# One attention stage of a six-stage decoder: the second norm's statistics taken from the first's, and weight splits cut in quarters

## The reference, cut to what matters

```python
def _layernorm(x, axis=-1, eps=1e-05):
    m = jnp.mean(x, axis=axis, keepdims=True)
    v = jnp.var(x, axis=axis, keepdims=True)
    return (x - m) / jnp.sqrt(v + eps)
...
x = _layernorm(x + _L0_attn_ref(x, L0_attn_Wq, L0_attn_Wk, L0_attn_Wv, L0_attn_Wo, L0_attn_scale), axis=-1)
x = _layernorm(x + _L0_xattn_ref(x, ctx_1024, L0_xattn_ln_gamma, L0_xattn_ln_beta, L0_xattn_w_q, L0_xattn_w_kv, L0_xattn_w_out, L0_xattn_b_out, L0_xattn_gate), axis=-1)
```

## Time and profile before

| what | value |
|---|---|
| median of 3 runs | 1186.19 us (1182.67 to 1187.83) |
| the profiled execution, its own time | 1185.38 us |
| its span | 1183.4 us |
| mean granted clock of TensorE | 0.961 |
| busy: PE, DVE, ACT, POOL | 1011.8, 891.5, 660.6, 567.9 us |

### The profile page before, as it was taken

How to read it: one execution, slowest core, us unless ns; L and a number is a source line. 1 busy time by engine, 2 the same in 40 slices (tenths; PEclk the granted TensorE clock), 3 DMA queues, 4 the chain that set the end, 5 groups by cost and what they waited for, 6 DMA issues and landing times.

```text
span 1183.4 us, 24998 instructions
## 1 busy us (share of the span) xinstructions
PE 1011.8 (85%) x8412; PEld 850.7 (72%) x8429; DVE 891.5 (75%) x2472; ACT 660.6 (56%) x2644; POOL 567.9 (48%) x671
## 2 busy tenths in 40 slices
PE   6998976799999999988999789977798676899984
PEld 2664655687788888767777689976687565788873
DVE  6899976677777777787777567659879566799885
ACT  5998974555555555554555354432553344666753
POOL 2677784333333333334883312758502684345452
PEclk9999988899999999999999899988999888999998
DMA  5510104400000000000111026432210110000000
GB/s 188 200 29 19 29 10 147 134 2 1 2 1 1 1 2 2 1 1 6 35 35 35 29 72 214 120 84 63 55 39 23 38 34 8 2 10 11 15 19 23
DMA packets 55604, 51.47 MB, mean 43 GB/s; under 512 B 6813, under 2 KB 48949, under 8 KB 55093
## 3 DMA queue, kind: packets, MB, share of 16 engines
q1 hardware_dynamic: 29556, 30.20, 8.0%
q10 hardware_dynamic: 21824, 11.28, 3.2%
q0 software_dynamic: 4096, 8.40, 2.5%
HBM read 29.66 MB, written 16.52 MB: 39 GB/s over the span
## 4 chain that ended last, share of the span: by engine, by line
PE 40%; DVE 27%; POOL 13%; issue 10%; ACT 6%; DMA 2%; ACTq 1%; DVEq 1%; SPq 0%; POOLq 0%
PE bank L672 34%; PE bank L687 6%; POOL xs L1752 5%; ACT PP L1466 3%; POOL GA L1770 3%; DVE X L1029 3%; DVE MX L1052 3%; POOL PP L1691 2%; DVE VB L1023 1%; DVE AC L1026 1%; DVE STA L1037 1%; ACTq L1552 1%; DVE X L1026 1%; DVE OT L1023 1%; DVE ED L1032 1%
## 5 line engine op out<-in xcount | busy, mean ns | idle before, releaser
L1466 ACT ACTIVATE PP<-bank,MX 128x128 f32<-128x128 f32 x832 | 296.2, 379 | 249.4 <-DVE MX L1052 227.1
L1691 POOL TENSOR_TENSOR PP<-PP,RS 128x512 f32<-128x512 f32 x208 | 215.8, 1045 | 219.2 <-DVE RS L1120 218.9
L1466 ACT ACTIVATION_READ_ACCUMULATOR PP<-bank,MX 128x1 f32 x832 | 178.4, 217 | 0.0
L1052 DVE TENSOR_REDUCE MX<-bank 128x4 f32<-128x512 f32 x208 | 141.1, 679 | 22.8 <-PE bank L672 18.6
L687 PE MATMUL bank<-KON,PP 128*128 128x128 f32 x832 | 135.4, 286 | 22.7 <-DVE PT L1023 13.5
L687 PEld LDWEIGHTS bank<-KON,PP 128*128 128x128 f32 x832 | 93.1, 143 | 58.3 <-issue 43.5
L672 PE MATMUL bank<-XST,WS 128*128 128x128 f32 x936 | 120.6, 280 | 2.8 <-ACT XST L1454 2.8
L672 PEld LDWEIGHTS bank<-XST,WS 128*128 128x128 f32 x936 | 114.0, 197 | 3.3 <-ACT XST L1454 3.3
L1023 DVE COPY PT<-bank 128x512 f32<-128x512 f32 x128 | 87.7, 685 | 12.7 <-PE bank L687 5.3
L1057 DVE COPY WS<-WCt 128x1152 f32 x78 | 64.6, 829 | 39.2 <-PE bank L672 28.7
L1752 POOL DMA_INDIRECT xs<-X,POS x64 | 67.7, 1058 | 49.8 <-DVE POS L1023 31.7
(11 more groups left out here) (259 smaller groups left out, 2472.6 us busy)
## 6 DMA issues: line engine op xcount, KB each, us to landing
xs<-BTZ ACTq DMA_DIRECT2D x2, 2496.0 KB, 18.8
XS<-xs SPq DMA_DIRECT2D x78, 64.0 KB, 1.9
ys<-YS ACTq DMA_DIRECT2D x78, 64.0 KB, 1.5
WFt<-wf SPq DMA_DIRECT2D x8, 515.0 KB, 5.0
KB<-KS SPq DMA_DIRECT2D x56, 64.0 KB, 2.0
WCt<-we SPq DMA_DIRECT2D x1, 3072.0 KB, 11.4
XT<-xT SPq DMA_DIRECT2D x8, 256.0 KB, 5.8
X<-x SPq DMA_DIRECT2D x8, 256.0 KB, 6.0
```

Source lines behind the costliest of these rows:

```text
L1052: e.tensor_reduce(m["MX"][:, u % d, :], heads(sb), AX.X, ALU.max, negate=True).then_inc(s["sm_max"], 1)
L1466: ins = e.activation(m["PP"][i][:, j, :], sb[:, one(j)], ACT.Exp, bias=m["MX"][:, i, j:j + 1], accum_out=m["SM"][:, i, j:j + 1])
L1691: return e.tensor_tensor(o, x, y, op)
```

## The change

The second norm's mean is 0, and its variance follows from the first's: with v the variance of z, the normalised row has v / (v + eps), and both norms together divide by the root of v(1 + eps) + eps². So `A_out` now makes two columns on VectorE (v + eps and v(1 + eps) + eps²), GpSimd raises both in one instruction, and one step `A_ln` writes XH and X, both from z. `A_ln2` is gone, and so are 32 `bn_stats` and 32 `bn_aggr`. The lags are now 8 (`A_out`), 10 (`A_ln`) and 12 (`A_xn`): all three fall on even i. `B_w` becomes 12 steps of a quarter (256 columns) at i = 22, 24, ... 44, `B_wv` four at i = 56 to 59, and `B_parts` 1 moves from 57 to 61. `B_wob` stays.

```diff
+WQK_AT = tuple(range(22, 46, 2))
+WV_AT = tuple(range(2 * NB - 8, 2 * NB - 4))
...
     def a_tail(i):
-        for name, lag in (("A_xn", 13), ("A_ln2", 11), ("A_ln", 9), ("A_out", 8)):
+        for name, lag in (("A_xn", 12), ("A_ln", 10), ("A_out", 8)):
...
-        if i in (27, 31, 35):
-            do("B_w", (27, 31, 35).index(i))
+        if i in WQK_AT:
+            do("B_w", WQK_AT.index(i))
...
+        if i in WV_AT:
+            do("B_wv", WV_AT.index(i))
+        if i == nu - 3:
+            do("B_parts", 1)
         if i == nu - 7:
             do("B_parts", 0)
-            do("B_wv")
-            do("B_parts", 1)
...
@@ TensorE
         elif name == "B_q":
             c, n = k
-            q.wait_ge("B_wl", 2)
+            q.wait_ge("B_wl", 8)
             q.wait_ge("B_lo", hi_lo(c)[1])
...
         elif name == "B_v":
             c, n = k
-            q.wait_ge("B_lo", max(hi_lo(c)[1], 3))
+            q.wait_ge("B_wl", 12)
+            q.wait_ge("B_lo", hi_lo(c)[1])
...
@@ VectorE
         e.bn_aggr(mv[:, 0:2], st).then_inc(s["ln_dv"], 1)
         q.wait_ge("ln_dv", 3 * n - 1)
+        if ty == "A":
+            ts(mv[:, 3:4], mv[:, 1:2], 1.0 + EPS, EPS * EPS, ALU.mult, ALU.add)
         ts(mv[:, 2:3], mv[:, 1:2], EPS, None, ALU.add).then_inc(s["ln_dv"], 1)
...
         elif name == "A_ln":
             b, = k
-            apply(X[:, b, :], X[:, b, :], "A1", b).then_inc(s["A_x1"], 1)
-            q.wait_ge("A_x1", b + 1)
-            stats("A2", b, X[:, b, :])
-        elif name == "A_ln2":
-            b, = k
+            mv = m["MVA"][:, b % 4, :]
+            q.wait_ge("ln_pw", N["A", b])
             q.wait_ge("A_xt", max(b - 3, 0))
-            apply(m["XH"][b % 4], X[:, b, :], "A2", b).then_inc(s["A_xh"], 1)
+            chain("A_xh", b + 1, ts(m["XH"][b % 4], X[:, b, :], mv[:, 0:1], mv[:, 5:6], ALU.subtract, ALU.mult))
+            ts(X[:, b, :], X[:, b, :], mv[:, 0:1], mv[:, 4:5], ALU.subtract, ALU.mult).then_inc(s["A_x1"], 1)
...
@@ ScalarE
+        elif name == "B_w" and k[0] % 3 < 2:
+            n, w = quarter(k[0] // 3), k[0] % 3
             q.wait_ge("ld_B", 96)
+            if w == 0:
+                e.activation(m["WQH"][:, n], m["WQB"][:, n], ACT.Copy, scale=0.125).then_inc(s["B_wh"], 1)
+            else:
+                cp(m["WKH"][:, n], m["WKB"][:, n]).then_inc(s["B_wh"], 1)
...
@@ GpSimd
+        if ty == "A":
+            tt(mv[:, 4:6], mv[:, 2:4], m["SW"][:, 0:2], ALU.pow).then_inc(s["ln_pw"], 1)
...
+            if w == 0:
+                q.wait_ge("B_wh", 2 * (k[0] // 3) + 1)
+                e.tensor_scalar(m["WQB"][:, n], m["WQB"][:, n], 0.125, None, ALU.mult).then_inc(s["B_wsc"], 1)
             else:
+                q.wait_ge("B_wh", 2 * (k[0] // 3) + w)
+                q.wait_ge("B_wsc", k[0] // 3 + 1)
+                x = ("WQ", "WK")[w - 1]
+                tt(m[x + "L"][:, n], m[x + "B"][:, n], m[x + "H"][:, n].bitcast(F32), ALU.subtract).then_inc(s["B_wl"], 1)
...
         elif name == "B_wv":
+            n = quarter(k[0])
+            q.wait_ge("B_wh", 9 + k[0])
+            tt(m["WVL"][:, n], m["WVB"][:, n], m["WVH"][:, n].bitcast(F32), ALU.subtract).then_inc(s["B_wl"], 1)
```

More of the change, by code:

```diff
@@ L458, in norms @@
 def norms(steps):
-    first = {"A_out": "A1", "A_ln": "A2", "B_out": "B", "combine": "C", "F_st": "F"}
+    first = {"A_out": "A", "B_out": "B", "combine": "C", "F_st": "F"}
     out = {}
@@ L590, in memory @@
         m[n] = at(n, 24)[:, :].rearrange("p (k j) -> p k j", k=6)
-    for n in ("A1", "A2", "B", "C", "D", "E", "F"):
+    m["MVA"] = at("MVA", 24)[:, :].rearrange("p (k j) -> p k j", k=4)
+    for n in ("A", "B", "C", "D", "E", "F"):
         m["ST" + n] = [at(f"ST{n}{i}", 6)[:, :] for i in range(2)]
-        m["MV" + n] = at(f"MV{n}", 16)[:, :].rearrange("p (k j) -> p k j", k=4)
+        if n != "A":
+            m["MV" + n] = at(f"MV{n}", 16)[:, :].rearrange("p (k j) -> p k j", k=4)
     m["XH"] = [at(f"XH{i}", 128)[:, :] for i in range(4)]
@@ L645, in hi_lo, with quarter @@
 def hi_lo(c):
-    return (1, 2) if c == 0 else (2 * c + 2, 2 * c + 3)
+    return 2 * c + 1, 2 * c + 2
+def quarter(n):
+    return slice(256 * n, 256 * n + 256)
 def par(m, k):
@@ L1509, in act @@
             cp(m["PT"][u % 3], heads(bank[(2, 6)[u % 2]])).then_inc(s["pt_act"], 1)
-        elif name == "B_w" and k[0] > 0:
-            n, = k
-            q.wait_ge("B_wsc", 1)
+        elif name == "B_w" and k[0] % 3 < 2:
+            n, w = quarter(k[0] // 3), k[0] % 3
             q.wait_ge("ld_B", 96)
-            cp(m[("WQH", "WKH")[n - 1]], m[("WQB", "WKB")[n - 1]]).then_inc(s["B_wh"], 1)
+            if w == 0:
+                e.activation(m["WQH"][:, n], m["WQB"][:, n], ACT.Copy, scale=0.125).then_inc(s["B_wh"], 1)
+            else:
+                cp(m["WKH"][:, n], m["WKB"][:, n]).then_inc(s["B_wh"], 1)
         elif name == "B_parts":
@@ L1526, in act @@
         elif name == "B_wv":
-            cp(m["WVH"], m["WVB"]).then_inc(s["B_hi"], 1)
+            q.wait_ge("ld_B", 96)
+            q.wait_ge("sm_s", 56)
+            cp(m["WVH"][:, quarter(k[0])], m["WVB"][:, quarter(k[0])]).then_inc(s["B_wh"], 1)
         elif name == "B_q" and k[1] % 2 == 1:
@@ L1696, in power @@
         q.wait_ge("ln_dv", 3 * N[ty, b])
-        tt(mv[:, 3:4], mv[:, 2:3], m["SW"][:, 0:1], ALU.pow).then_inc(s["ln_pw"], 1)
+        if ty == "A":
+            tt(mv[:, 4:6], mv[:, 2:4], m["SW"][:, 0:2], ALU.pow).then_inc(s["ln_pw"], 1)
+        else:
+            tt(mv[:, 3:4], mv[:, 2:3], m["SW"][:, 0:1], ALU.pow).then_inc(s["ln_pw"], 1)
     for step in steps:
@@ L1710, in pool @@
         elif name == "A_out":
-            power("A1", k[0])
+            power("A", k[0])
         elif name == "A_ln":
-            power("A2", k[0])
-        elif name == "A_ln2":
             b, = k
-            q.wait_ge("A_xh", b + 1)
+            q.wait_ge("A_x1", b + 1)
             q.wait_ge("B_bt", 1)
@@ L1719, in pool @@
         elif name == "B_w":
-            n, = k
+            n, w = quarter(k[0] // 3), k[0] % 3
             q.wait_ge("ld_B", 96)
-            if n == 0:
-                e.tensor_scalar(m["WQB"], m["WQB"], 0.125, None, ALU.mult).then_inc(s["B_wsc"], 1)
-            else:
-                q.wait_ge("B_wh", n)
-                tt(m[("WQL", "WKL")[n - 1]], m[("WQB", "WKB")[n - 1]], m[("WQH", "WKH")[n - 1]].bitcast(F32), ALU.subtract
-                   ).then_inc(s["B_wl"], 1)
+            if w == 0:
+                q.wait_ge("B_wh", 2 * (k[0] // 3) + 1)
+                e.tensor_scalar(m["WQB"][:, n], m["WQB"][:, n], 0.125, None, ALU.mult).then_inc(s["B_wsc"], 1)
+            else:
+                q.wait_ge("B_wh", 2 * (k[0] // 3) + w)
+                q.wait_ge("B_wsc", k[0] // 3 + 1)
+                x = ("WQ", "WK")[w - 1]
+                tt(m[x + "L"][:, n], m[x + "B"][:, n], m[x + "H"][:, n].bitcast(F32), ALU.subtract).then_inc(s["B_wl"], 1)
         elif name == "B_wob":
```

6 lines of the change are left out of this document (2 added, 4 removed).

## The result

The changed kernel takes 1199.2 us (median of 7 runs, 1194.23 to 1202.36), the kernel before 1187.83 us in the same comparison (7 runs, 1182.67 to 1194.46). The ratio is 1.0077, with a 95% interval of 1.0041 to 1.0112: slower by 0.8 %. The forecast was 1194.0 in a range of 1178 to 1203. The profiled execution is the longest of the seven: 1202.36 us, span 1200.5 us, granted clock 0.958.

A forecast was written before the change was run, and what follows sets the result against it. VectorE's own work was taken to set stage A's row at 4.84 us, just above a closed chain of waits. 6.7 + 1.8 - 0.5 = +8.0 on the profiled 1185.4 gives 1193.4, with 0.8 for the median 1194 us; range 1178 to 1203.

The forecast's parts named there:

- The closed chain: Stage A: waits from one even unit's scores to the next grow from 4.68 to 5.69 us a row.
- hand-over: Bank 7, stage A: `A_out` waits until VectorE takes out XH's transpose, 0.31 + 0.55 = 0.86 us a row.
- Over units 12 to 54: Stage A, 21 rows at 5.69 us: 119.5 us against 112.8 before, +6.7 us.
- Quarters at nothing: Stage A: splitting in quarters costs nothing; in rows under 4.7 us up to 0.27 us each.
- That `B_wob` fits into the slack: Stage A: GpSimd's scaling in `B_wob`, nearly 2.8 us, fits its row's slack, so that row is no longer.
- From unit 54 to B: Unit 54 to B's first scores: hand-over +6.9, other waits -1.5, slow clock -3.0, first `B_q` -0.6; sum +1.8 us.
- both slow-clock stretches: Unit 54 to B: two stretches at half the granted clock, 1.5 us each, would go: -3.0 us.
- The start of B: B's first steps: rows 31 and 30 finish with fewer statistics ahead of the maxima, -0.5 us.
- Rival 1: Stage A: hand-over stays out of the chain, rows take 4.68 plus 0.08 us; total 1170 us, chance 0.17.
- Rival 2: Stage A: the hand-over costs half, 0.43 us a row; total 1182 us, no change; chance 0.13.
- Rival 3: TensorE's clock: four more slow stretches at 1.5 us each give 1200 us; chance 0.10.
- Rival 4: Stage A: two-column powers might cost more than one, or the wait on them still bite; given no time of its own.

The follow-up runs named there:

- first experiment: The changed kernel with only the lag of `A_xn` put back from 12 to 13 (transposition on odd units): 1214.27 us, ratio 0.9971 to the kernel before.
- second experiments: The kernel before with only the lag of `A_xn` raised from 13 to 14 (transposition on the even unit): 1246.73 us, ratio 1.0244.
- sixth experiment: The changed kernel with `B_w` and `B_wv` whole and placed as before the change: 1232.01 us, ratio 1.0122 to the kernel before.
- tenth experiment: The eighth's kernel with the two zero-fill transfers issued by SyncE instead of ScalarE: 1194.31 us, ratio 0.9769 to the kernel before.
- fifth experiments: The changed kernel again, unedited, on another chip: 1231.73 us, ratio 1.0115 to the kernel before.
- The eighth: The first experiment's kernel with GpSimd's quarter moved ahead of the next row's power: 1208.28 us, ratio 0.9906 to the kernel before.

## Why the prediction was right, and where it wasn't

*The closed chain.* Right, in mechanism and size. 5.69 us a row were added up from links measured in other places; the rows take 5.66. The hand-over costs 0.31 + 0.56 = 0.87 (forecast 0.86), `A_out`'s link 0.72 (0.72). The extra column is 0.13 from the first of the pair to QA rather than 0.16, and the first and second experiments show that the transposition's place alone makes and unmakes it: 4.72 without it on the even unit, 5.83 with it in the old kernel. The prediction followed the longer of two paths, rightly. The shared bank by itself is a smaller part than it reads there: 0.25 of the 0.94 us in this kernel by the estimate at the first experiment, and the rest stands on VectorE. The views that I named as proof show what they should: VectorE at 78 % (I had said under 85), 2408 instructions on it for 2472, which is 64 fewer, the idle time ahead of `A_out` ended by XT and that ahead of the projection by QA or KS.

*Over units 12 to 54.* Forecast +6.7, measured +6.35.

*Quarters at nothing.* Right in this kernel, and right on what happens when the cover goes, but the price was wrong. I had bounded it by ScalarE's copy, up to 0.27 us a row. In rows of 4.7 to 4.8 it was 0.2 to 0.9, through GpSimd and VectorE: the step "ScalarE's quarter can be bounded by the VA copy" looked at the wrong engine. The row that should have told me is in the earlier trace rows: X with 1.06 us for an instruction that takes 0.34 elsewhere. I read the burst as a wait for the power alone. XH is as slow a little earlier in the same row:

```profile
86.09 0.98 DVE L1029 TENSOR_SCALAR XH<-X,MVA 128x128 f32<-128x128 f32 x1
```

So of the burst's 1.91 us the wait for the power is 0.47, and the two slow norm instructions are 0.64 + 0.72 = 1.36.

*That `B_wob` fits into the slack.* Right in the number, and lucky. The row is 5.66 like the others (with lag 13 it is 5.35), but I had looked at the power alone, and put at nothing that the scaling runs beside VectorE's norm. XH met WOB where it is let through; WQB in rows of the same length, met 1 us later, costs 1.06 us (sixth experiment).

*From unit 54 to B.* Forecast +1.8, measured +3.1. I had dropped both slow-clock stretches (-3.0); one of them is still there, behind the first `B_q`, whose own wait is 2.50 instead of 3.20 (forecast -0.6, measured -0.7). I had said that most of this wait stays, and should have kept the clock's fall with it: 1.5 of my 3.0. With it the term would have been +3.3.

*The start of B.* The forecast was -0.5 and the measurement +1.7, so the sign was wrong. 0.45 of it is ScalarE's longer gap in the zero fill. Most of the rest is TensorE's longer waits just behind it: `A_out` of the last row starts behind the fill there (221.52), since the transposition ahead of it on bank 7 (205.97) gets its XT only at 219.62; before it started at 197.68, ahead of the stall. The fill wasn't in my account at all. It is the largest single wait of this stretch in both kernels, and the tenth experiment shows it to be worth 14.5 us, as much as the hand-over's whole loss up to B's steady rows (first and fifth experiments: 6.6 ahead and 8.0 behind the kernel before, 14.6 us apart, or 17.2 without the row of unit 18). That the issue takes longer after this change isn't shown: in the fifth and eighth runs ScalarE's gap was 13.1 us, close to before's 12.89.

*The total.* 8.0 forecast; 8.56 at B's first scores, 10.3 at its steady rows, 11.4 between the medians. What lies behind the steady rows is in stages without a difference in their instructions. The runs don't settle it.

*The rivals.* Rival 1 (4.68 + 0.08 = 4.76 a row if the hand-over isn't in the chain) describes the first experiment, with 4.72. It was a good picture of what the new norm can do and not of this change. It would have given 1170 only if the quarters had cost nothing in short rows; they did cost, and the first experiment gained 0.3 % instead of 1.3. The eighth, where the twelve quarters cost nothing, gained 0.9. Rival 2 is excluded by the 0.87. Its formula, and the 0.3 us that bounds the hand-over from below, also left VectorE's order out: behind XT stand XH and X, so a cheaper hand-over alone would have brought the row to 5.66 - 0.25 = 5.41 us and no lower (by the same estimate). Rival 3: at an even 5.66 us with TensorE busy for 85 %, the granted clock stayed at 1.00 in the stretches shown; the fall at 174.49 came right after a wait of 2.50 us. I had misread its ground, though. Of the three falls in the rows of stage A before, only the last followed a long wait (3.20 us); those at about 115 and 153 us came behind two waits each, of 0.58 and 1.00, and of 1.03 and 1.02 us. The Trainium skill ("TensorE: Matmul & The Clock Gate", section on what is actually happening) says that activity releases the throttle, and I had taken from it that even waits are a risk. At even waits of up to 0.6 us the trace shows none. Rival 4: the power of two columns takes 0.70 us instead of 2 x 0.55.
